# Count stage of a graph network kernel: which engine makes which 128-column comparison, and when ScalarE computes its distances

## The reference

```python
edge_index = jnp.stack([src, dst])
x = _layernorm(x + _L0_gnn_ref(x, edge_index, L0_gnn_W1, ...), axis=-1)
...
def gcn_conv(x, edge_index, W, b):
    n = x.shape[0]
    loop = jnp.arange(n)
    src = jnp.concatenate([edge_index[0], loop])
    dst = jnp.concatenate([edge_index[1], loop])
    xw = x @ W.T
    deg = jax.ops.segment_sum(jnp.ones_like(dst, dtype=x.dtype), dst, num_segments=n)
    dinv = jnp.where(deg > 0, jax.lax.rsqrt(deg), 0.0)
    norm = dinv[src] * dinv[dst]
    msg = xw[src] * norm[:, None]
    out = jax.ops.segment_sum(msg, dst, num_segments=n)
    return out + b
```

## Time and profile before

| | us |
|---|---|
| median of 3 runs (4216.05 to 4226.9) | 4219.95 |
| the profiled execution | 4214.28 |
| its span in the trace | 4212.5 |
| VectorE busy in the span | 3092.9 |
| TensorE busy | 2836.2 |
| GpSimd busy | 2666.3 |
| ScalarE busy | 2403.7 |

### The profile page before, as it was taken

One profiled execution on the slowest core, in us unless ns is written; L12 is line 12 of the kernel. 1 busy time (PEld: TensorE's weight loads), 2 busy tenths in 40 slices (PEclk: granted clock), 3 DMA queues, 4 the chain that ended last, 5 costly groups with the idle time before them and its releaser, 6 DMA issues. The chain is left out here.

```text
span 4212.5 us, 58543 instructions
## 1 busy us (share of the span) xinstructions
PE 2836.2 (67%) x16208; PEld 1802.9 (43%) x16208; DVE 3092.9 (73%) x9684; ACT 2403.7 (57%) x5241; POOL 2666.3 (63%) x2801
## 2 busy tenths in 40 slices
PE   1899998974576766764546767676635676766763
PEld 1344445543354544543334535444423354544542
DVE  6999994564576776778667877777855676776785
ACT  1888882005566666662646656666365566666644
POOL 5766660305777777773577777777347777777743
PEclk8999999986788888987678888889857888888886
DMA  3111112632222222221232223323112222222210
GB/s 104 56 83 83 59 80 96 227 134 61 64 69 69 68 69 69 65 69 29 52 71 70 66 70 70 71 70 71 27 40 64 69 69 68 68 69 68 66 48 16
DMA packets 127620, 298.57 MB, mean 71 GB/s; under 512 B 45412, under 2 KB 74972, under 8 KB 123712
## 3 DMA queue, kind: packets, MB, share of 16 engines
q0 software_dynamic: 74976, 155.58, 16.3%
q1 hardware_dynamic: 52320, 139.24, 9.8%
HBM read 241.28 MB, written 53.38 MB: 70 GB/s over the span
## 5 line engine op out<-in xcount | busy, mean ns | idle before, releaser
L1416 POOL DMA_INDIRECT work<-table,lane_src x2184 | 2092.5, 958 | 665.3 <-issue 644.6
L1513 PE MATMUL psum<-work 128*128 128x396 bf16 (+1 forms) x5850 | 1162.9, 354 | 67.1 <-ACT work L1458 32.1
L1455 ACT ACTIVATE work<-work,middle_node_number 128x384 f16<-128x384 f16 x1587 | 954.4, 601 | 225.2 <-PE psum L1513 205.0
L1458 ACT ACTIVATE work<-work 128x384 bf16<-128x384 f16 x1587 | 829.7, 523 | 50.5
L1570 PE MATMUL psum<-work 128*128 128x136 f32 x4836 | 701.4, 303 | 186.2 <-DVE work L1701 95.2
L1513 PEld LDWEIGHTS psum<-work 128*128 128x128 bf16 x5850 | 597.5, 104 | 511.6 <-issue 122.3
L1570 PEld LDWEIGHTS psum<-work 128*128 128x128 f32 x4836 | 653.5, 208 | 272.2 <-issue 159.1
L1738 DVE TENSOR_TENSOR node_sums<-node_sums,psum 128x136 f32 x2418 | 558.0, 292 | 105.2 <-PE psum L1570 98.1
L793 POOL TENSOR_SCALAR work<-work 128x128 f16<-128x128 f16 x392 | 335.5, 857 | 220.3 <-PE psum L808 193.0
L771 DVE TENSOR_SCALAR work<-work 128x400 f16<-128x400 f16 x1568 | 461.2, 316 | 1.4 <-PE psum L808 0.8
L741 PE MATMUL psum<-work 128*128 128x448 f16 x2100 | 451.4, 352 | 3.2 <-PEq L1166 2.5
(11 more groups left out here) (374 smaller groups left out, 2927.5 us busy)
## 6 DMA issues: line engine op xcount, KB each, us to landing
counts<-work SPq DMA_DIRECT2D x14, 2800.0 KB, 8.3
work<-counts SPq DMA_DIRECT2D x14, 2800.0 KB, 9.8
work<-table,lane_src POOLq DMA_INDIRECT x2184, 2.5
work<-spread SPq DMA_DIRECT2D x78, 256.0 KB, 4.0
work<-masks SPq DMA_DIRECT2D x78, 128.0 KB, 3.0
work<-source_rows SPq DMA_DIRECT2D x39, 192.0 KB, 3.7
spread<-node_sums SPq DMA_DIRECT2D x4, 896.0 KB, 9.0
table<-work SPq DMA_DIRECT2D x10, 330.0 KB, 3.0
```

The costliest lines, as they stand in the source:

```text
L1416: pool.indirect_dma_start(m.ring[:, s % SLOTS, 0:F + H], None, m.d_table[H], bass.IndirectOffsetOnAxis(ap=m.src[:, s:s + 1], axis=0)).then ...
L1455: act.activation(away, rows_of(g, u), ACT.Abs, bias=m.low_tile[:, hi:hi + 1]).then_inc(far_known, 1)
L1458: act.activation(hot_of(g, u), away, ACT.Relu, bias=1.0, scale=-1.0).then_inc(hot_act, 1)
L1513: mm = pe.matmul(aid_banks[:, k, 0:3 * (F + H)], hot_of(g, u)[:, k * P:(k + 1) * P], m.all_thirds[:, :, hi, 0:F + H], start=(hi == 0), sto ...
```

## The change

`PAIRED`, the number of `hot_lo` that GpSimd makes, becomes a function of the unit: two (tiles 0 and 1) in an even unit, one (tile 0) in an odd one. VectorE makes what is left: tile 2 in an even unit, tiles 1 and 2 in an odd one. GpSimd still signals once a unit, behind its last instruction.

On ScalarE the distance of unit n + 3 now stands ahead of the relu of unit n + 2; before, both were of unit n + 2. A wait for the relu of the previous unit (`lo_hot`) stands ahead of it, since the two distance buffers are used in turn. The loop over chunks is written in another form with the same waits and copies.

```diff
--- before.py
+++ after.py
@@ -72,7 +72,6 @@
 CG = -(-CUNITS // P)
 CCOLS = NODE_TILES * CW
 DEPTH = 4
-PAIRED = 1
 LEAD = 2
 ARENA = 33280
 F16 = mybir.dt.float16
@@ -282,7 +281,7 @@
     assert late <= ARENA
     late = 4 * 8 * LANES + 8 * P
     m.lo_away = m.arena[:, late:late + P].bitcast(F16).rearrange("p (d c) -> p d c", d=2)
-    assert CUNITS + LEAD <= CG * P and CHUNK % CREGS == 0
+    assert CUNITS + LEAD + 1 <= CG * P and CHUNK % CREGS == 0
     m.agg = [t.rearrange("p j f -> p (j f)")[:, 0:NPAD + CW] for t in (m.acc, m.acc_odd)]
 
 
@@ -752,6 +751,9 @@
     stored = (stored0, stored1)
     dinv_blocks = [(j, min(j + 8, NODE_TILES)) for j in range(0, NODE_TILES, 8)]
 
+    def paired(n):
+        return 2 - n % 2
+
     def unit_bank(k):
         return m.ps[k % 4 // 2][:, k % 2 * 512:k % 2 * 512 + CCOLS]
 
@@ -766,7 +768,7 @@
                         dve.wait_ge(unit_done, n - (DEPTH - 1))
                     d = k % DEPTH
                     for b in range(CB):
-                        if PAIRED <= b < CB - 1:
+                        if paired(n) <= b < CB - 1:
                             dve.tensor_scalar(m.hot_lo[:, d, b, :], m.iota_cols[:, 0:P], m.low[:, b, n:n + 1], None, ALU.is_equal)
                         t = dve.tensor_scalar(m.hot_key[:, d, b, :], m.iota_cols[:], m.key[:, b, n:n + 1], None, ALU.is_equal)
                     t.then_inc(hot, 1)
@@ -789,7 +791,7 @@
             for n in range(CUNITS):
                 if n >= DEPTH:
                     pool.wait_ge(unit_done, n - (DEPTH - 1))
-                for b in range(PAIRED):
+                for b in range(paired(n)):
                     t = pool.tensor_scalar(m.hot_lo[:, n % DEPTH, b, :], m.iota_cols[:, 0:P], m.low[:, b, n:n + 1], None, ALU.is_equal)
                 t.then_inc(lo_paired, 1)
 
@@ -832,32 +834,32 @@
 
         @block.scalar
         def _(act):
-            def last_low(n, k):
-
+            def distance(n):
+                act.activation(m.lo_away[:, n % 2, :], m.iota_cols[:, 0:P], ACT.Abs, bias=m.low_last[:, n:n + 1], scale=-1.0).then_inc(lo_away, 1)
+
+            def last_low(n):
                 if n >= DEPTH:
                     act.wait_ge(unit_done, n - (DEPTH - 1))
-                away = m.lo_away[:, k % 2, :]
-                act.activation(away, m.iota_cols[:, 0:P], ACT.Abs, bias=m.low_last[:, n:n + 1], scale=-1.0).then_inc(lo_away, 1)
                 act.wait_ge(lo_away, n + 1)
-                act.activation(m.hot_lo[:, k % DEPTH, CB - 1, :], away, ACT.Relu, bias=1.0, scale=-1.0).then_inc(lo_hot, 1)
-
-            def chunk(c, q, i):
+                act.activation(m.hot_lo[:, n % DEPTH, CB - 1, :], m.lo_away[:, n % 2, :], ACT.Relu, bias=1.0, scale=-1.0).then_inc(lo_hot, 1)
+
+            distance(0)
+            for n in range(LEAD):
+                if n:
+                    act.wait_ge(lo_hot, n)
+                distance(n + 1)
+                last_low(n)
+            for c in range(CHUNKS):
                 if c >= 2:
-
-                    act.wait_ge(stored[q], i * 16)
+                    act.wait_ge(stored[c % 2], c // 2 * 16)
                     act.wait_ge(produced, c - 1)
                 for k in range(CHUNK):
-                    last_low(c * CHUNK + (k + LEAD), k + LEAD)
-                    act.wait_ge(unit_done, c * CHUNK + (k + 1))
-                    act.copy(m.counts[q][:, k, :], unit_bank(k)).then_inc(evacuated, 1)
-
-            for k in range(LEAD):
-                last_low(k, k)
-            chunk(0, 0, 0)
-            chunk(1, 1, 0)
-            for i in range(1, CHUNKS // 2):
-                chunk(i * 2, 0, i)
-                chunk(i * 2 + 1, 1, i)
+                    n = c * CHUNK + k
+                    act.wait_ge(lo_hot, n + LEAD)
+                    distance(n + LEAD + 1)
+                    last_low(n + LEAD)
+                    act.wait_ge(unit_done, n + 1)
+                    act.copy(m.counts[c % 2][:, k, :], unit_bank(k)).then_inc(evacuated, 1)
             for n, (lo, hi) in enumerate(dinv_blocks):
                 act.wait_ge(dinv_turned, n + 1)
                 act.copy(m.dinv_row[:, lo * P:hi * P], m.ps[n % 2][:, 0:(hi - lo) * P]).then_inc(dinv_taken, 1)
```

## The result

The changed kernel takes 4239.36 us (median, 4237.4 to 4245.52), the kernel before 4216.05 us next to it: a ratio of 1.0053, 95% interval 1.0040 to 1.0066. It is slower by 23 us, as forecast in its sign, but by less than half of the 53 us that I gave. The time lies inside my range, and the reason I gave for it was wrong.

What follows compares the result with a forecast made beforehand. VectorE was taken to bound the count stage, with GpSimd becoming the bound after the change: +45 us from the third chunk on and +7 before, together +53, on 4214.3 gave 4267 us; range 4186 to 4330.

Steps and rivals of the forecast that it cites:

- ScalarE costs nothing: Count stage: ScalarE's three instructions take 1.205 us a unit, under 1.26 of the fastest case, so its reordering was costed at nothing.
- the upper bound: Count stage: VectorE's saving alone, without hindrance from GpSimd, is worth 0.097 x 336 + about 7 = 40 us.
- The two engines hold each other up: Count stage: GpSimd either gets turns at 0.79 us, costing VectorE 0.094 each, or about one turn per VectorE unit.
- The mild sum: Count stage: VectorE pays 0.094 us per GpSimd instruction; 2.80 a pair, 1.40 a unit, 1.32 in the first two chunks.
- I take the middle of the two: Count stage: halfway between mild and hard sums, 1.49 us a unit from the third chunk on, 1.48 before; +53 us.
- The hard way: Count stage: GpSimd's third turn runs in VectorE's idle time; 3.17 a pair, 1.585 a unit, 1.635 in the first two chunks.
- the sign of being wrong: Count stage: the forecast fails if GpSimd's back-to-back instructions stay under 0.87 us next to a VectorE that never waits.
- VectorE would have idle time and TensorE would wait for GpSimd: Count stage: with GpSimd as the bound, VectorE's saving is worth nothing and TensorE's waits for GpSimd reach tens of us.
- rival B: Count stage: the mild way everywhere, VectorE busy throughout at 1.35 to 1.40 us a unit, about +13 us; chance 0.22.
- A: Count stage, the forecast case: GpSimd is the bound, kernel slower, own range 4228 to 4339 us; chance 0.50.
- Rival D: TensorE's clock in the count stage could fall again with longer waits, adding to A within its upper end; no own chance.
- rival C: Count stage: GpSimd's turns fall into gaps of VectorE, 1.305 us a unit, total -22 us, 4192; chance 0.28.

Runs made afterwards that it cites:

- e3: The changed kernel with GpSimd's second comparison of an even unit left out from the fifth unit on, made by nobody: 5635.81 us, 21 us under before.
- e1: The changed kernel with GpSimd making one comparison in every unit as before, only ScalarE's distance one unit ahead: ratio 0.9998 to before.
- e7: The changed kernel with each of GpSimd's three comparisons a pair waiting for one of VectorE's 400-column comparisons: 4208.7 us, 8 us under before.
- e4: The kernel before with one more GpSimd comparison in each even unit, into a spare buffer, VectorE's work unchanged: 5680.3 us, 24 us over before.
- e10: The changed kernel with VectorE's one 128-column comparison of an even unit moved to the front: 5751.44 us, 27 us over before.
- e9: The changed kernel with two comparisons of every unit on GpSimd and one on VectorE: 4227.45 us, 11 us over before.
- e5: The changed kernel with GpSimd's second comparison of an even unit put behind the wait for the odd unit: 4209.22 us, ratio 0.9983 to before.
- e6: The changed kernel with each of GpSimd's three comparisons a pair waiting for a product of its own on TensorE: 4203.84 us, ratio 0.9970 to before.
- e11: The changed kernel with VectorE's 128-column comparison of an even unit moved behind the first 400-column one: 5745.74 us, 21 us over before.

## Why the prediction was right in its sign and wrong in its size

- **VectorE is the bound, and 0.163 us a pair leaves it.** Right: e3 shows the pair at 2.58.
- **ScalarE costs nothing.** Right: e1 at 0.9998. TensorE is close behind too, but its 1.26 a unit is a little high: in the second chunk of e7 it goes without idle time at 1.24 (18.66 us for the 15 units from 150.00 to 168.66). And "about 7" in the upper bound should be 75.7 - 56 x 1.18 = 9.6; nothing hangs on it.
- **TensorE waited for GpSimd once, 0.2 us.** Misread: this is what the profile puts down to GpSimd. In ten units of the first chunk of before, GpSimd ended behind VectorE, by up to 3.05 us (134.28 against 131.23), and in seven of them TensorE began 0.1 us behind GpSimd's end. It changes nothing from the second chunk on, where GpSimd is 3.4 us ahead.
- **The two engines hold each other up.** Right, and this alone is the slowdown. The mild sum was the near one: 2.80 a pair against the measured 2.87, from a price of 0.094 for an instruction against 0.116; in the first two chunks it gave 1.32, measured are 1.34 and 1.31.
- **The step that failed is "I take the middle of the two".** The hard way, GpSimd at 1.4 to 2.2 us an instruction and VectorE waiting for it, got half the weight in all 392 units from 19 instructions of the first chunk of before. In the changed kernel it never shows: none of its 588 comparisons takes over 1.16 us, the three of a pair stand back to back at 0.67 each, under the 0.87 that I had named as the sign of being wrong, and its first 28 units are the ones that got faster. Four of the thirteen traces have the hard state (before, e1, e4 and e10), all of them in the first two chunks and none later; it ended for good at one wait of VectorE in the first three and came back twice in e10. So the change from one way to the other that I read in the earlier trace rows is real, but no trace shows it in the 336 units to which I carried it. Half the weight on it made +53 where the mild sum alone had +13 and the measured is +23; the 10 us between the last two are the mild price, sized too low (1.40 a unit against 1.433). Why some kernels fall into the state and others don't stays open.
- **VectorE would have idle time and TensorE would wait for GpSimd.** Wrong, by the waits above. From the third chunk on the second half holds only with four comparisons a pair (e9), and the first half in no kernel. So the profile is that of rival B, somewhat over its 1.35 to 1.40, and it is luck that the time lies inside the range of A. Rival D did not come either: from 145 us on the granted clock is 1.00, the higher of its two levels, as before.
- **What the mild price is.** I treated it as a number per instruction. Its size is off by little (0.094 to 0.116), but the idea is wrong: with 13 VectorE instructions a pair and three of GpSimd the pair took 2.66 (e5, e6), 2.70 (e7), 2.79 (e10, e11) and 2.87 (changed kernel), prices from 0.14 to 0.35. The rival C, a gain of about 20 us if the turns fall well, is in part what e6 shows with its 13 us; the change as written doesn't let them fall well.

The Trainium skill's rule of one shared pair of ports ("SBUF — State Buffer", section "SBUF: two separate sides") had the direction of the change right. Its "fully blocks" is not seen: VectorE loses 0.02 to 0.12 us on average for a GpSimd instruction of 0.6 to 0.9, 0.02 for a single one of before.

What stays open: why one place costs 0.02 and another 0.12. The runs show that it goes by where GpSimd's instructions fall in VectorE's order (e5 has the same three in a row as the changed kernel, one unit later, and pays 0.14 instead of 0.35); which part of an instruction holds the other up they do not show.

## What to carry to other kernels

When work is moved from a busy VectorE to an idle GpSimd, the idle time of GpSimd is not the budget: count what VectorE loses for each GpSimd instruction beside it, from its start-to-start times with and without one. That loss depends on where the instructions fall, so a wait that releases them elsewhere (the odd unit's in e5, a semaphore of TensorE's products in e6) can turn a loss of 0.5% into a gain of 0.3% with the same work. And a bad stretch at the start of a stage is carried over only to units in which the engines do the same in the same order; these first chunks lack the addition of 16 columns on VectorE. That this is what keeps the state away later was not tested.

## What the runs showed of the hardware that I had not expected

- A GpSimd comparison of 128x128 float16 beside a VectorE that never idles took 0.60 to 1.16 us, most of them under 0.92, and 1.4 to 2.4 us in one state, in which VectorE ran almost undisturbed until it had to wait for a buffer.
- With two comparisons on GpSimd in every unit (e9) neither engine waited in 400 us, and they kept the same pace without it: GpSimd's end stayed 0.14 to 0.46 us behind VectorE's from the first unit to the last.
- VectorE with 0.163 us less work a pair and the same three GpSimd instructions ran at the same pace (1.432 in the changed kernel, 1.430 in e4), and with one more comparison moved to GpSimd in each odd unit faster than both (1.391 in e9).
- Where no addition of 16 columns stands in VectorE's order (first two chunks), the same release points gave other prices: 1.24 us a unit with VectorE's pace, 1.385 with e5's, which was among the best from the third chunk on.
